# Moving four feed-forward products of the first batch, and taking row statistics tile by tile, in a macaron transformer layer

## The reference

```python
x = x + 0.5 * ffn(layernorm(x))
x = x + attn(layernorm(x))
x = x + 0.5 * ffn(layernorm(x))
```

## Time and profile before

| what | value |
|---|---|
| median of 3 runs | 615.34 us (614.55 to 616.1) |
| the profiled execution | 612.61 us |
| its span, first to last instruction | 610.8 us |
| PE busy, share of the span | 550.3 us, 90% |
| DVE | 409.0 us, 67% |
| ACT | 310.6 us, 51% |
| POOL | 240.6 us, 39% |
| mean granted TensorE clock | 0.975 |

### The profile page before, as it was taken

One profiled execution on the slowest core, in us unless ns is written; L12 is line 12 of the kernel. 1 busy time (PEld: TensorE's weight loads), 2 busy tenths in 40 slices (PEclk: granted clock), 3 DMA queues, 4 the chain that ended last, 5 costly groups with the idle time before them and its releaser, 6 DMA issues.

```text
span 610.8 us, 10067 instructions
## 1 busy us (share of the span) xinstructions
PE 550.3 (90%) x3586; PEld 234.5 (38%) x3586; DVE 409.0 (67%) x782; ACT 310.6 (51%) x629; POOL 240.6 (39%) x200
## 2 busy tenths in 40 slices
PE   0698987997989999999999999999998999998867
PEld 0443534533433343343343343343343333343432
DVE  5889686768877677677677677677567712522562
ACT  0832535212246667567566667667556565652330
POOL 4004656524565655655655655655401100100100
PEclk9799899798999999999999999999999999999997
DMA  9912123241612243413213217242400030101011
GB/s 311 381 72 78 53 83 116 79 165 40 170 60 80 78 123 114 146 53 117 75 53 115 76 54 251 78 122 79 147 1 2 2 137 31 41 18 47 7 69 69
DMA packets 43601, 57.95 MB, mean 95 GB/s; under 512 B 3526, under 2 KB 34374, under 8 KB 42528
## 3 DMA queue, kind: packets, MB, share of 16 engines
q1 hardware_dynamic: 42972, 57.21, 28.5%
q10 hardware_dynamic: 580, 0.11, 0.1%
HBM read 32.01 MB, written 25.17 MB: 94 GB/s over the span
## 4 chain that ended last, share of the span: by engine, by line
PE 65%; DVE 21%; issue 4%; ACT 4%; POOL 3%; DMA 2%; SPq 0%; ACTq 0%; POOLq 0%; DVEq 0%
PE bank L1077 10%; PE bank L977 9%; PE bank L939 9%; PE bank L957 8%; PE bank L1087 8%; PE bank L889 8%; PE bank L899 6%; DVE rmax L830 4%; PE bank L1017 3%; DVE stats L672 3%; DVE mparts L843 2%; PE bank L879 2%; DVE big L687 2%; DVE wl L738 2%; DVE rmax L840 2%
## 5 line engine op out<-in xcount | busy, mean ns | idle before, releaser
L830 DVE TENSOR_REDUCE rmax<-bank 128x1 f32<-128x512 f32 (+3 forms) x384 | 199.3, 552 | 96.3 <-PE bank L957 93.3
L620 ACT ACTIVATE big<-bank 128x512 f32<-128x512 f32 (+3 forms) x384 | 181.6, 492 | 131.9 <-PE bank L939 127.8
L957 PE MATMUL bank<-kst,qst 104*128 104x512 f16 (+3 forms) x384 | 125.4, 330 | 10.2 <-DVE rmax L830 9.8
L939 PE MATMUL bank<-qst,kst 106*128 106x512 f16 (+3 forms) x384 | 125.7, 329 | 3.1 <-ACT big L620 2.8
L515 POOL TENSOR_TENSOR rot<-t,sin_s 64x512 f32<-64x512 f32 x64 | 83.0, 1296 | 80.6 <-ACT t L613 77.7
L1077 PE MATMUL bank<-big,ones 128*32 128x512 f32 (+3 forms) x768 | 81.8, 498 | 0.0
L1087 PE MATMUL bank<-big,rows 128*32 128x512 f32 (+3 forms) x768 | 79.5, 486 | 0.0
L939 PEld LDWEIGHTS bank<-qst,kst 106*128 106x128 f16 x384 | 36.8, 96 | 90.6 <-issue 39.3
L524 POOL TENSOR_TENSOR rhl<-t,rhl 128x512 f16<-128x512 f32 x32 | 37.6, 1175 | 62.2 <-ACT rhl L634 62.2
L957 PEld LDWEIGHTS bank<-kst,qst 104*128 104x128 f16 x384 | 37.8, 98 | 46.7 <-DVE rmax L830 16.1
L534 POOL TENSOR_TENSOR cl<-cf,ch 128x512 f16<-128x512 f32 x16 | 18.8, 1175 | 93.0 <-ACT ch L652 93.0
(11 more groups left out here) (106 smaller groups left out, 698.9 us busy)
## 6 DMA issues: line engine op xcount, KB each, us to landing
spread<-rhl SPq DMA_DIRECT2D x32, 256.0 KB, 2.2
qst<-spread SPq DMA_DIRECT2D x16, 384.0 KB, 3.7
kst<-spread SPq DMA_DIRECT2D x16, 384.0 KB, 3.9
x<-rows SPq DMA_DIRECT2D x4, 1024.0 KB, 4.3
spread<-rhl SPq DMA_DIRECT2D x32, 128.0 KB, 2.1
rows<-in_L_attn_x_dram SPq DMA_DIRECT2D x3, 1024.0 KB, 14.2
xh<-ch SPq DMA_DIRECT2D x4, 512.0 KB, 5.6
xl<-cl SPq DMA_DIRECT2D x4, 512.0 KB, 6.7
```

What stands on the lines that cost most here:

```text
L620: nc.scalar.activation(probs[:, st % P_PLACES, h, 0:n], pb[u % 2][:, 0:n], ACT.Exp, scale=EXP_SCALE).then_inc(s_eb, 1)
L830: nc.vector.tensor_reduce(rmax[:, at:at + 1], a_bank(u)[:, 0:n], AX.X, ALU.max, negate=True).then_inc(s_max, 1)
L939: nc.tensor.matmul(pb[u % 2][:, 0:n], kst[0:ROWS_B, g % SETS, h, j * P:(j + 1) * P], qst[0:ROWS_B, g % SETS, h, q0:q0 + n], start=True, st ...
L957: nc.tensor.matmul(a_bank(u)[:, 0:n], qst[0:ROWS_A, g % SETS, h, i * P:(i + 1) * P], kst[0:ROWS_A, g % SETS, h, half * HALF:half * HALF + ...
```

## The change

Products 4 to 7 of the first batch's last feed-forward leave the loop. 4 and 5 are placed right behind the loop, before the second batch's output tiles 4 to 7; 6 and 7 behind product 3 of the second batch. So that they can wait, the second batch's feed-forward uses `ch` and `cl` for its columns instead of `xh` and `xl`, and other banks. Product 3 of the second batch moves behind the transposes of its second half. The output tiles wait for the high part first and for the low part only before their fifth matmul. And `statistics` is taken apart: `tile_statistics` stands right behind the update of each tile, behind a wait for that update, and `gather` (the rest of `statistics`) where `statistics` stood. This holds for the first batch's first half in the first feed-forward, for both halves of the second batch there, and for all of the statistics after the attention. DVE's updates, SP's stores and the four `weight_low` of the first weight follow the new order.

```diff
-        y3_bank = [bank[0:2] * 4, [bank[i] for i in (3, 4, 6, 3, 6, 3, 4, 6)]]
-        f3_bank = [bank[0:2] * 4, [bank[i] for i in (4, 6, 3, 4, 3, 4, 6, 3)]]
+        y3_bank = [bank[0:2] * 4, [bank[i] for i in (3, 4, 6, 3, 2, 7, 5, 2)]]
+        f3_bank = [bank[0:2] * 4, [bank[i] for i in (4, 6, 3, 4, 6, 3, 4, 6)]]
...
-        F3_STEP = [O0_START + 80 + 4 * r for r in range(4)] + [O0_START + 107 + 4 * r for r in range(4)]
+        F3_STEP = [O0_START + 80 + 4 * r for r in range(4)]
...
-            for r in range(TILES):
-                if F3_STEP[r] + 7 >= LAST_STEP:
-                    store(0, r)
-            for r in range(TILES):
+            store(0, 4)
+            store(0, 5)
+            for r in range(4):
+                store(1, r)
+            store(0, 6)
+            store(0, 7)
+            for r in range(4, TILES):
                 store(1, r)
...
                 if b:
-                    act.wait_ge(s_ffn3[0], 4 * bl + 4)
+                    act.wait_ge(s_o[1], 4 * bl + 4)
...
-                scale_shift(y3_bank[b][n], xh[:, cc, bl * HALF:(bl + 1) * HALF], f3[b][bl][:, cc, :], s_f3[b])
+                scale_shift(y3_bank[b][n], (xh, ch)[b][:, cc, bl * HALF:(bl + 1) * HALF], f3[b][bl][:, cc, :], s_f3[b])
...
+            def tile_statistics(bl, r, src):
+
+                nc.vector.bn_stats(stats[:, 4 * bl + r, :], src[:, r, :]).then_inc(s_link, 1)
+                links[0] += 1
...
-            ffn_update(0, f1_bank[0], blocks[0], s_ffn1[0], s_up1[0])
...
+            for r in range(4):
+                ffn_update(r, f1_bank[0], blocks[0], s_ffn1[0], s_up1[0])
+                dve.wait_ge(s_up1[0], r + 1)
+                tile_statistics(0, r, blocks[0][0])
+                if r < 3:
+                    weight_low(0, r)
+            gather(0, 0, 3, *ONCE)
+            weight_low(0, 3)
...
                         ffn_update(n, f1_bank[1], blocks[1], s_ffn1[1], s_up1[1])
+                        dve.wait_ge(s_up1[1], n + 1)
+                        tile_statistics(n // 4, n % 4, blocks[1][n // 4])
...
-                        dve.wait_ge(s_oup[0], 4 * bl + 4)
-                        statistics(0, bl, 9 + bl, *TWICE, resid[0][bl])
+                        gather(0, bl, 9 + bl, *TWICE)
...
                     attention_update(o[0], o[1])
+                    dve.wait_ge(s_oup[o[0]], o[1] + 1)
+                    tile_statistics(o[1] // 4, o[1] % 4, resid[o[0]][o[1] // 4])
...
-            dve.wait_ge(s_oup[1], 4)
-            statistics(1, 0, 11, *TWICE, resid[1][0])
+            gather(1, 0, 11, *TWICE)
+            ffn_update(4, f3_bank[0], resid[0], s_ffn3[0], s_up3[0])
             normalize(1, 0, 11, resid[1][0], y3[1][0], s_y3[1])
-            attention_update(1, 4)
-            attention_update(1, 5)
-            attention_update(1, 6)
+            ffn_update(5, f3_bank[0], resid[0], s_ffn3[0], s_up3[0])
+            for r in range(4, 7):
+                attention_update(1, r)
+                dve.wait_ge(s_oup[1], r + 1)
+                tile_statistics(1, r - 4, resid[1][1])
             for n in range(4):
-                f_low(n, f3[1], xh, xl, s_f3[1], s_fl3[1])
+                f_low(n, f3[1], ch, cl, s_f3[1], s_fl3[1])
             attention_update(1, 7)
             dve.wait_ge(s_oup[1], 8)
-            statistics(1, 1, 12, *TWICE, resid[1][1])
+            tile_statistics(1, 3, resid[1][1])
+            gather(1, 1, 12, *TWICE)
+            ffn_update(0, f3_bank[1], resid[1], s_ffn3[1], s_up3[1])
             normalize(1, 1, 12, resid[1][1], y3[1][1], s_y3[1])
-            for r in range(4):
-                ffn_update(r, f3_bank[1], resid[1], s_ffn3[1], s_up3[1])
-            for n in range(4, 8):
-                f_low(n, f3[1], xh, xl, s_f3[1], s_fl3[1])
+            ffn_update(1, f3_bank[1], resid[1], s_ffn3[1], s_up3[1])
+            ffn_update(2, f3_bank[1], resid[1], s_ffn3[1], s_up3[1])
+            f_low(4, f3[1], ch, cl, s_f3[1], s_fl3[1])
+            ffn_update(3, f3_bank[1], resid[1], s_ffn3[1], s_up3[1])
+            f_low(5, f3[1], ch, cl, s_f3[1], s_fl3[1])
+            ffn_update(6, f3_bank[0], resid[0], s_ffn3[0], s_up3[0])
+            f_low(6, f3[1], ch, cl, s_f3[1], s_fl3[1])
+            f_low(7, f3[1], ch, cl, s_f3[1], s_fl3[1])
+            ffn_update(7, f3_bank[0], resid[0], s_ffn3[0], s_up3[0])
...
-            pe.wait_ge(s_cl, 2 * ALL)
+
+            def late_product(r):
+
+                if r >= 6:
+                    pe.wait_ge(s_up3[0], r - 1)
+                product(f3_bank[0][r], r, xh, xl, range(9), s_ffn3[0])
+
+            pe.wait_ge(s_fl3[0], 8)
+            late_product(4)
+            late_product(5)
             for r in range(4, TILES):
                 pe.wait_ge(s_oup[1], r - 1)
-                output_products(1, r, range(3 * GROUPS))
+                pe.wait_ge(s_ch, 2 * ALL)
+                output_products(1, r, range(GROUPS))
+                pe.wait_ge(s_cl, 2 * ALL)
+                output_products(1, r, range(GROUPS, 3 * GROUPS))
...
-            for r in range(4):
-                if r == 3:
-                    pe.wait_ge(s_up3[1], 1)
-                product(f3_bank[1][r], r, xh, xl, range(9), s_ffn3[1])
+            for r in range(3):
+                product(f3_bank[1][r], r, ch, cl, range(9), s_ffn3[1])
             pe.wait_ge(s_y3[1], 8)
             for cc in range(CC):
-                if cc < 3:
-                    pe.wait_ge(s_up3[1], cc + 2)
-                else:
+                if cc == 3:
                     pe.wait_ge(s_f3[1], 5)
                 transposed(y3_bank[1][4 + cc], y3[1][1], cc, s_ytr3[1])
+            pe.wait_ge(s_up3[1], 1)
+            product(f3_bank[1][3], 3, ch, cl, range(9), s_ffn3[1])
+            late_product(6)
+            late_product(7)
             pe.wait_ge(s_fl3[1], 8)
             for r in range(4, TILES):
-                if r == 7:
-                    pe.wait_ge(s_up3[1], 5)
-                product(f3_bank[1][r], r, xh, xl, range(9), s_ffn3[1])
+                pe.wait_ge(s_up3[1], r - 2)
+                product(f3_bank[1][r], r, ch, cl, range(9), s_ffn3[1])
```

More of the change, by code:

```diff
@@ L671, in statistics, with gather @@
                         dve.wait_ge(s_xtile[r], 16)
-                    last = nc.vector.bn_stats(stats[:, 4 * bl + r, :], src[:, r, :])
-                    last = last.then_inc(s_link, 1)
-                    links[0] += 1
+                    tile_statistics(bl, r, src)
+                gather(b, bl, n, mul, add)
+            def gather(b, bl, n, mul, add):
                 dve.wait_ge(s_link, links[0])
@@ L807, in _ @@
                         f_low(n, f3[0], xh, xl, s_f3[0], s_fl3[0])
-                    if k == F3_STEP[n] + 3:
+                    if n < 4 and k == F3_STEP[n] + 3:
                         ffn_update(n, f3_bank[0], resid[0], s_ffn3[0], s_up3[0])
@@ L811, in _ @@
                     if k == S2_STEP[bl]:
-                        dve.wait_ge(s_up1[1], 4 * bl + 4)
-                        statistics(1, bl, 7 + bl, *ONCE, blocks[1][bl])
+                        gather(1, bl, 7 + bl, *ONCE)
                     if k == N2_STEP[bl]:
@@ L1099, in _ @@
                                         ident16[:, :]).then_inc(s_mtr, 1)
-            for r in range(TILES):
-                if F3_STEP[r] + 3 > LAST_STEP:
-                    raise AssertionError(r)
-            pe.wait_ge(s_cl, 2 * ALL)
+            def late_product(r):
[5 more added lines that the diff above has]
+            late_product(5)
             for r in range(4, TILES):
                 pe.wait_ge(s_oup[1], r - 1)
-                output_products(1, r, range(3 * GROUPS))
+                pe.wait_ge(s_ch, 2 * ALL)
+                output_products(1, r, range(GROUPS))
+                pe.wait_ge(s_cl, 2 * ALL)
+                output_products(1, r, range(GROUPS, 3 * GROUPS))
                 if r == 5:
```

## The result

The changed kernel takes 596.25 us (median of 4 runs, 595.52 to 597.19); the kernel before, run beside it, 615.54 us (4 runs, 614.55 to 616.1). The ratio is 0.9689, with an interval of 0.9668 to 0.971. The profiled execution took 596.86 us (span 595.1), which is 15.75 us less than the profiled 612.61 us of before, where the sum of the forecast's steps was 14.9.

A forecast was written before the change was run, and what follows sets the result against it. The kernel was taken as bound by PE, except where PE waits for another engine. Product placing -11.36 and statistics -3.5 gave -14.9 us, 612.61 to 597.7; with the 2.73 us offset 600.5 us, range 597 to 605.5.

The forecast's parts named there:

- -7.76: Loop stage where PE is always busy: four products of 1.94 us leave it, -7.76 us.
- 0.36: Wait for `cl` behind the loop: products 4 and 5 take 3.88 us, the filled wait was 3.52, so +0.36 us.
- 0.72: PE's wait at 580.59: one `tile_statistics` (0.6) and its wait (0.12) now precede the four `f_low`, +0.72 us.
- 1.74: Tail, first to fifth product of the second batch: 14.45 us instead of 16.19, late products 6 and 7 included, -1.74 us.
- the rival in which exponentials take over there: Emptied loop stage: PE waits for exponentials or output sums; half of 7.76 lost 604.4 us, all lost 608; chance 0.1.
- L1097's wait of 3.10 us: Listed sign of being wrong: L957 or L1097 waiting as long as before behind other DVE work.
- The rival in which only the products pay: At 137 and 473 us PE meets the next wait, or added DVE steps cancel the gain: -11.4, 604 us; chance 0.2.
- The added steps on DVE: Loop updates each have 0.72 us more behind them, delaying score maxima; taken 0, bounds 0 and +2 us.
- the same offset: Median of the runs, 615.34, lies 2.73 us above the profiled execution; carried over from 597.7 to forecast 600.5 us.
- the term for the clock: Tail, 596.78 to 605.54 us: with the 4.3 us hole filled, three products take 5.82 instead of 8.76 us, -2.94.
- The rival of a clock that falls all the same: Tail: clock falls at the longer `f_low` wait or bank wait, three products slow again, +2.94, 603.4 us; chance 0.12.
- The rival "more than forecast": From 133 to 150 us: the clock, 0.90 there, also holds, worth 1.7 us: 598.8 us; chance 0.06.

The follow-up runs named there:

- e7: Changed kernel with the second batch's tile 6 statistic moved behind the four `f_low`: 594.7 us, ratio 0.9693 to the kernel before.
- e2: Kernel before with statistics taken tile by tile, all products where they were: 608.61 us, ratio 0.9912 to the kernel before.
- e5: Changed kernel, unchanged, run again beside the kernel before on another chip: 596.62 us against 613.76, ratio 0.9717.
- e9: Kernel before, unchanged, traced a third time: 615.02 us in one execution.
- e11: Changed kernel, unchanged, traced a third time: 596.21 us in one execution.
- e6: Kernel before with 15 and 18 unused matmuls in PE's waits for `cl` and the last `f_low`, nothing moved: 611.09 us, ratio 0.9949.
- e1: Kernel before, unchanged, run and traced again: 614.74 us against 613.95 for its other runs on that chip, ratio 1.0009.

## Why the prediction was right, and where it was wrong

**The tail, right.** The terms were -7.76 + 0.36 + 0.72 - 1.74 - 2.94 for the products and -0.1 for statistics, -11.46 us; against the trace from which they were read it is 116.36 - 104.94 = -11.42. The single terms hold too. From 569.42 to 583.92 pass 14.50 us, forecast 14.45. The `f_low` wait grew from 0.60 to 1.32, forecast +0.72; e7 took it back by moving one instruction. The products end 0.23 us after `cl`, as worked out: POOL's `cl` runs from 553.55 for 1.16 us, to 554.71, and output tile 4 starts at 554.94. PE stays full in the emptied loop stage (9.30 of 9.30 us), so the rival in which exponentials take over there falls.

**Statistics, right.** First batch's output projection: -1.77 in the first trace (26.98 to 25.21), forecast -1.8; its second half: PE's wait at the transposes behind the normalization went from 0.99 to 0.85 us, -0.14, forecast -0.1. Second batch's second half: from the first to the second `mrows` every trace without tile statistics takes 17.6 us and every one with them 15.8, so -1.8, forecast -1.6. It is the 1.42 us that went; that L1097's wait of 3.10 us stays had been named as a sign of being wrong, but the -1.6 did not count on it. The rival in which only the products pay falls with e2. The added steps on DVE took nothing in the long middle of the loop: 307.5 to 308.5 us in all thirteen traces.

**The failed step: "with the same offset I forecast 600.5 us".** I read the median's 2.73 us above the profiled execution as scatter that would ride along with any kernel, and added it to the 597.7 us that the terms gave. That is most of the miss: from 600.5 to 596.25 it is 2.7 for the offset, 0.9 by which the traced execution of the changed kernel lies under the terms' 597.7, and 0.6 by which its median lies under that. The runs showed what the offset is. Three further traces of before lie 2.1 to 2.4 us above the first, and the difference sits behind PE's waits: +1.4 behind the score maxima, +1.1 behind the statistics, +2.8 behind `cl`, less 1.2 because the hole cost 1.7 instead of 2.9 us. That is 4.1; 1.5 to 1.9 us earlier starts in those traces, before the first `mrows`, take a part back. The change removes or fills three of these waits, and at the maxima 1.1 of the 1.4 us go although the 3.10 us stay; so the offset goes too. It was the clock, and the trace that I had was a lucky one from the maxima to `cl`, though not at its hole nor at its start. PE's timeline of the first batch's first products in that trace, then in e5; the last row of each is the third product's start:

```profile
26.74 0.59 PE L886 MATMUL bank<-bias_rows,ones 128*128 128x512 f16 x1 [1.73 <-DVE xl L695]
...
33.55 0.38 PE L886 MATMUL bank<-bias_rows,ones 128*128 128x512 f16 x1
```

```profile
27.11 0.38 PE L906 MATMUL bank<-bias_rows,ones 128*128 128x512 f16 x1 [1.59 <-DVE xl L706]
...
30.99 0.38 PE L906 MATMUL bank<-bias_rows,ones 128*128 128x512 f16 x1
```

The first two take 6.81 us in the first trace and 5.5 to 5.8 in the three others of before. Over the thirteen traces the two go with the first `mrows`: 3.88 us in the four that reach it at 125.2 to 125.7 us, 5.2 to 5.9 in the eight from 126.1 to 127.4, 6.81 in the one at 128.02.

With it the term for the clock was mis-sized. I took 2.94 us, for the hole alone. Against the three later traces of before it is 1.1 + 1.1 + 2.8 + 1.7 = 6.7 us (of the 1.4 behind the maxima, 1.1 are gone: from the second to the third `mrows` e9 takes 15.4 us and the changed kernel 14.3). With -8.42 for the products as forecast and -3.7 for statistics as measured it makes -18.8 us. From e9 to e11, on the same chip, it is 615.02 - 596.21 = 18.8. In the two stages of the loop (2.9 us each) the terms were read from such traces themselves, so their sum had to come out. In the tail it is a test: 8.42 forecast, 0.14 for statistics and 4.5 for the clock make 13.1, and 13.1 were measured. e6 shows the clock's share of the tail by itself, without any work moved.

One sentence of evidence was weaker than it looked: that the clock stayed at 1.00 past waits of like length. For the like waits, 0.60 and 1.37 us, it holds in all four traces of before. But behind 1.78 us in the loop the clock falls in three of the four, which the one trace could not show, so little room was left above the 1.32 us of the changed kernel. The rival of a clock that falls all the same still lost: no wait of the changed kernel behind the loop is over 1.32 us, and the clock is 1.00 from 478 to 584 us in three traces.

**The rival "more than forecast"** (598.8 us) had the right sign and the wrong place. In the changed kernel the clock behind the score maxima is still 0.88 (142.78 to 157.07 us), hardly other than in the first trace (0.89); only against the 0.81 of e9 is it a gain.

**Open.** What decides in one execution whether the clock falls behind a wait of 1.8 or 3.5 us was not tried, nor why the first two products are slow in some executions and not in others, nor why 1.1 us at the maxima go with the tile statistics. Traces of before were four; how often its clock falls in the other executions is not counted, and on the chips of e1 and e5 its median (613.95 and 613.76) lies only 1.2 to 1.3 us above the first trace. So it is not settled why the gain is 19.3 us by the first comparison's medians and 17.1 by e5's: the changed kernel has 596.25 and 596.62 there, the kernel before 615.54 and 613.76.

## What to carry to other kernels

Where PE waits for a few us, price the wait twice, as its length and as the half-speed matmuls that can follow it; and look for the second price in more than one profiled execution, since a single one can lack it. An offset of the median over the profiled execution is not a constant of the chip: before carrying it over to a changed kernel, ask which event makes it and whether the change removes that event. Independent products put into the waits pay both prices at once, and a few filler matmuls pay the second one alone.

## What was not expected of the hardware

- The same wait in the same program leaves the granted clock alone in one execution and halves it in others: 3.52 us at `cl`, clock 1.00 from 567 to 576 us in one trace and 0.64 to 0.67 in three; 1.78 us at the statistics, 1.00 in one and 0.86 in three. Even a PE wait under 2 us was followed by a fall to the lower of the two levels (1.2 of 2.4 GHz): in e9 eight matmuls take 1.95 us where they take 1.04 in the first trace.
- The fall behind the hole costs 1.4 to 2.9 us: 3.36 to 3.64 us for one product, or two products at 6.82 together in the first trace.
- A wait of DVE for its own last instruction again goes with 0.11 us: in the changed kernel an update at 550.80 is followed by its statistic at 551.52, 0.72 later, while a statistic is followed by an instruction that does not wait for it 0.61 later (566.27 to 566.88), as in the earlier trace rows. No run takes such a wait away by itself.
